# The rotation's last addition moved from VectorE to GpSimd, four per batch at fixed places of its order

## The chip, the cores and the metric

The kernel runs on one core of one Trainium2 chip. The time is that of the device in microseconds (us), the median of several executions. A core has five engines that run side by side, each its own list of instructions in order: TensorE (PE), VectorE (DVE), ScalarE (ACT), GpSimd (POOL) and SyncE (SP), which here issues the DMAs. They wait for each other by semaphores.

## What is computed

One layer of cross attention and a quantised feed-forward on x of 16 x 256 x 512, in fp32. Cut to the attention, in which the change lies:

```python
q = rope((layernorm(x) @ Wq.T + bq))     # 16 heads of 32
k = rope((ctx @ Wk.T + bk));  v = ctx @ Wv.T + bv
probs = softmax(where(causal, q @ k.T / sqrt(32), -inf))
x = x + (probs @ v) @ Wo.T + bo
x = x + ffn(layernorm(x))                # 4-bit weights, 16-bit activations
# rope: x1, x2 are the halves of a head; the result is
# [x1*c - x2*s, x1*s + x2*c]
```

## The kernel before, in words

`attend` does the attention for 16 batches of 256 tokens; `feed_forward` follows it with barriers between. In `attend` the 16 heads of a batch are four groups of four (g = 0 to 3), and s = 4 * batch + g counts the groups over all batches.

The order on every engine is written out by hand, in a string of words for each: `PE_LINE`, `ACT_LINE`, `DVE_LINE`, `POOL_LINE` (lines 81 to 87), and a `..._BEGIN` string for the opening. `whole_plan` repeats a line for i = 1 to 18. A word is a step and a group, and "+1" or "-2" shifts its batch against i: `rope1+1` in line i is the rotation of group 1 of batch i+1, `stat2-2` the second statistics of batch i-2. Words whose batch does not exist fall out. An engine works on its words strictly in that order; a word that has to wait holds up all that stand behind it.

The words of one group, in the order of the data: QK (TensorE, queries and keys of a group), raw (ScalarE, L600 and L603, adds the biases into `raw`), rope (VectorE, L504 to L512), S (TensorE, scores, L716), max (VectorE, L515 and L516), exps (ScalarE, eight exponentials, L609), recip (VectorE, L520), norm (GpSimd, L413 and L415, divides by the sums), PT (TensorE, transposes, L738 and L743), pte (ScalarE), PV (TensorE), othi and otlo (ScalarE, VectorE). There is one set of score banks: S of a group waits for the exponentials of the group before (`exped`).

A rope is four VectorE instructions on 128 x 512 fp32: `by_sin` = raw * sin, `by_cos` = raw * cos, a shuffle of `by_sin` inside each head into `sin_turned`, and the addition `qk[g]` = `by_cos` + `sin_turned`, which counts up `rotated`; S waits for `rotated`.

GpSimd's other words: stat (statistics of the layer norm of x, four small operations, L371 to L375, after VectorE's bn), stat2 (the same for the second layer norm, after x2), res (x + bias, L402) and wdeq (a unit of feed-forward weights, L407; VectorE's wqa, wqb and wqc come before it). ScalarE's xn (L583) waits for stat, xn2 (L631) for stat2. xn0 and xn1 free the tile `x_in`, into which SyncE loads the next batch (L297); bn0 (L491) waits for that load.

The order of GpSimd's steady line is, for line i:

```python
POOL_LINE = "stat2-2 stat+2 norm3-1 norm0 res-1 wdeq norm1 norm2"
```

Of the kernel before, what the change touches and what calls it, by code (L numbers as in the profile page):

```python
# [5 lines left out]
ALU = mybir.AluOpType  # L6
# [18 lines left out]
GROUPS = HEADS // HG  # L25
# [11 lines left out]
HALF_TURN = [(k + HD // 2) % HD for k in range(HD)]  # L37
# [35 lines left out]
def split_scales(dve, link, dst_inv, dst_half, peak, power):  # L73
# [10 lines left out]
            "cthi1+2 ytev1-2 exps2 pte1 xthi0+2 raw1+1 whi othi1 pte2 exps3 othi2 xthi1+2 xn1+3 raw2+1")  # L84
DVE_LINE = ("otlo2-1 max0 wqb rope2 recip0 ctlo1+1 peak-2 otlo3-1 bn0+3 max1 wqc rope3 recip1 otlo0 max2 x2_0-1 "
            "rope0+1 bn1+3 xtlo0+2 recip2 x2_1-1 wlo otlo1 max3 ctlo0+2 rope1+1 recip3 wqa+1 xtlo1+2")
POOL_LINE = "stat2-2 stat+2 norm3-1 norm0 res-1 wdeq norm1 norm2"
GATE_STEPS = ("wqa", "wqb", "wqc", "wdeq", "WT", "whi", "wlo")


# [21 lines left out]
def whole_plan(begin, line, after):  # L112

    plan = steps_of_line(begin, 0)
    for i in range(1, BATCH + 3):
        for step in steps_of_line(line, i):
            plan.append(step)
            plan += after.get((i, step[0], step[1]), [])
    return plan


def counts_of(plan):

    made, count = {}, {}
    for name, g, b in plan:
        made[name] = made.get(name, 0) + 1
        count[name, g, b] = made[name]
    return count
# [8 lines left out]
             "bn0+1 bn1+1 max0 rope1 scale1 lo4 rope2 recip0 scanc1 join2 xtlo0+1 xtlo1+1 max1 scale2 lo5 ctlo0+1 ctlo1+1 "  # L137
             "rope3 recip1 bv bn0+2 bn1+2 max2 otlo0 rope0+1 bias recip2 bn0+3 bn1+3 max3 otlo1 xtlo0+2 rope1+1 recip3 "
             "ctlo0+2 xtlo1+2")
POOL_BEGIN = "stat stat+1 norm0 stat+2 norm1 norm2"  # L140
LATE_SETS = [(2 * k - 3, k) for k in range(2, BATCH // 2)]
PE_PLAN = whole_plan(PE_BEGIN, PE_LINE, {(i, "S", 2): [("MX", j, 0)] for i, j in
                                         [(i, k + 1) for i, k in LATE_SETS] + [(DOWN_SCAN + DOWN_SCANS, 9)]})
# [10 lines left out]
DVE_PLAN = whole_plan(DVE_BEGIN, DVE_LINE, DVE_AFTER)  # L154
POOL_PLAN = whole_plan(POOL_BEGIN, POOL_LINE, {})
PE_COUNT, ACT_COUNT, DVE_COUNT, POOL_COUNT = (counts_of(p) for p in (PE_PLAN, ACT_PLAN, DVE_PLAN, POOL_PLAN))
# [16 lines left out]
def attend(nc, io, keep):  # L173

    with ExitStack() as ctx:
        def buf(name, shape, dt):
            return ctx.enter_context(nc.sbuf_tensor(name, shape, dt))

        def sem(name):
            return ctx.enter_context(nc.semaphore(name))  # L180
# [7 lines left out]
        qk = qg(76, 8, F32, "p (g a t) -> p g a t", g=GROUPS, a=2)  # L188
# [25 lines left out]
        by_sin = buf("by_sin", [P, 2, SEQ], F32)  # L214
        by_cos = buf("by_cos", [P, 2, SEQ], F32)
        sin_turned = buf("sin_turned", [P, 2, SEQ], F32)
# [49 lines left out]
        filled = [sem(f"filled{b}") for b in range(RING)]  # L266
        emptied = [sem(f"emptied{b}") for b in range(RING)]
        x_hi, c_hi, c_ready, heads_hi = sem("x_hi"), sem("c_hi"), sem("c_ready"), sem("heads_hi")
        raw_used, rotated = sem("raw_used"), sem("rotated")
        scored, max_ready, exped, sums_ready = sem("scored"), sem("max_ready"), sem("exped"), sem("sums_ready")  # L270
        normed = sem("normed")
        w_in, w_rounded, w_hi = sem("w_in"), sem("w_rounded"), sem("w_hi")
# [14 lines left out]
        def await_free(eng, name, g, b, part=0):  # L287
            bank, n = BANK[name, g, b, part]
            eng.wait_ge(emptied[bank], n + 1)
            return bank  # L290
# [71 lines left out]
        @block.gpsimd  # L362
        def _(pool):
            steps = Tally()

            def link(ins):
                ins.then_inc(pool_step, 1)
                pool.wait_ge(pool_step, steps.next())

            def statistics(mo, rs, sh):  # L370
                pool.tensor_scalar(rs[:, :], mo[:, :, 1], LN_EPS, None, ALU.add).then_inc(pool_step, 1)  # L371
                steps.next()
                link(pool.tensor_scalar(sh[:, :], mo[:, :, 0], -1.0, None, ALU.mult))
                link(pool.tensor_tensor(rs[:, :], rs[:, :], minus_half[:, :], ALU.pow))
                return pool.tensor_tensor(sh[:, :], sh[:, :], rs[:, :], ALU.mult)  # L375

            link(pool.memset(ident[:, :], 0.0))
            link(pool.memset(ident_b[:, :], 0.0))
            link(pool.memset(mask[:, :], 0.0))
            link(pool.memset(minus_half[:, :], -0.5))  # L380
            pool.memset(ones[:, :], 1.0).then_inc(ident_ready, 1)
            pool.affine_select(out=ident[:, :], in_=ident[:, :], compare_op=ALU.not_equal, fill=1.0,
                               base=0, pattern=[[-1, P]], channel_multiplier=1).then_inc(ident_ready, 1)
            for name, g, i in POOL_PLAN:
                if name == "stat":
                    pool.wait_ge(var_ready, TT * (i + 1))
                    statistics(moments, rstd, shift).then_inc(stat_ready, 1)
                    if i == 0:
                        pool.affine_select(out=ident_b[:, :], in_=ident_b[:, :], compare_op=ALU.not_equal, fill=1.0,
                                           base=0, pattern=[[-1, P]], channel_multiplier=1).then_inc(ident_ready, 1)  # L390
                        for at in (0, P):
                            diag = mask[:, at:at + P]
                            pool.affine_select(out=diag, in_=diag, compare_op=ALU.is_ge, fill=MASKED,
                                               base=0, pattern=[[-1, P]], channel_multiplier=1).then_inc(ident_ready, 1)
                if name == "stat2":
                    pool.wait_ge(x2_ready, TT * (i + 1))
                    statistics(moments2, rstd2, shift2).then_inc(stat2_ready, 1)
                if name == "res":
                    pool.wait_ge(res_loaded, 16 * (i + 1))
                    if i == 0:  # L400
                        await_free(pool, "BIAS", 0, 0)
                    pool.tensor_tensor(x_res[:, :, :], x_res[:, :, :],  # L402
                                       bias_row[:, :].unsqueeze(1).to_broadcast([P, TT, D]), ALU.add).then_inc(xb_ready, 1)
                if name == "wdeq":
                    pool.wait_ge(w_rounded, i)
                    q = w_deq[:, :].rearrange("p (k j) -> p k j", j=QBLOCK)
                    pool.tensor_tensor(q, q, step[:, :].unsqueeze(2).to_broadcast([P, D // QBLOCK, QBLOCK]),  # L407
                                       ALU.mult).then_inc(w_dequantised, 1)
                if name == "norm":
                    s = i * GROUPS + g  # L410
                    pool.wait_ge(sums_ready, s + 1)
                    pr, ps = prob[:, s % 2], per_sum[:, s % 2]
                    pool.tensor_tensor(pr[:, :, 0:P], pr[:, :, 0:P],  # L413
                                       ps[:, 0, :].unsqueeze(2).to_broadcast([P, HG, P]), ALU.mult)
                    pool.tensor_tensor(pr[:, :, P:3 * P], pr[:, :, P:3 * P],  # L415
                                       ps[:, 1, :].unsqueeze(2).to_broadcast([P, HG, 2 * P]), ALU.mult).then_inc(normed, 1)

        @block.vector
        def _(dve):
            done = Tally()  # L420

            def link(ins):
                ins.then_inc(dve_step, 1)
                dve.wait_ge(dve_step, done.next())

            for name, g, i in DVE_PLAN:
                s = i * GROUPS + g
# [76 lines left out]
                if name == "rope":  # L504
                    await_free(dve, "QK", g, i)
                    if s == 0:
                        dve.wait_ge(consts_in, 16 * 3)
                    link(dve.tensor_tensor(by_sin[:, :, :], raw[:, s % 2], sin[:, :, :], ALU.mult))
                    dve.tensor_tensor(by_cos[:, :, :], raw[:, s % 2], cos[:, :, :], ALU.mult).then_inc(raw_used, 1)
                    link(dve.stream_shuffle(sin_turned[:, :, :].rearrange("p a t -> p (a t)"),  # L510
                                            by_sin[:, :, :].rearrange("p a t -> p (a t)"), HALF_TURN))
                    dve.tensor_tensor(qk[:, g], by_cos[:, :, :], sin_turned[:, :, :], ALU.add).then_inc(rotated, 1)  # L512
                if name == "max":
                    dve.wait_ge(scored, s + 1)
                    dve.tensor_reduce(neg_max[:, s % 2, 0, :], score_banks[:, :, 0:P], AX.X, ALU.max, negate=True)  # L515
# [951 lines left out]
```

## Time and profile before

| | |
|---|---|
| median of 3 runs | 1614.03 us (1614.02 to 1615.21) |
| the profiled execution | 1613.66 us |
| its span, first to last instruction | 1611.8 us |
| mean granted clock of TensorE | 0.947 |
| TensorE busy | 1394.6 us, 87% |
| VectorE busy | 1235.3 us, 77% |
| ScalarE busy | 921.6 us, 57% |
| GpSimd busy | 321.2 us |

The profile is one execution. Busy times are sums over an engine's instructions; an engine that is idle waits for what the profile names behind "<-" in square brackets, with the idle time in front of it. In the timelines each row is one instruction or a run of equal ones: when it starts, how long it takes, the engine, the line of the code, the operation, what it writes and reads, and the shapes. The attention stage covers about the first 720 us.

### The profile page before, as it was taken

How to read it: one execution, taken by the hardware profiler on the slowest of the kernel's cores; microseconds unless marked ns; L12 is line 12 of the kernel's file. 1: busy time of each engine (PE TensorE's matmuls, PEld its weight loads, DVE VectorE, ACT ScalarE, POOL GpSimd, SP SyncE). 2: the span in 40 equal slices, each digit the busy share in tenths (PEclk: the TensorE clock that was granted, in tenths of full speed). 3: DMA queues.
4: the chain of work that ended last, by engine and by line, in shares of the span. 5: the costliest groups of instructions: out<-in, count | busy, mean ns of one | idle time of the engine just before them, and what ended most of it. 6: DMA issues, size and time to landing. Idle time of an engine off the chain costs nothing.

```text
span 1611.8 us, 24568 instructions
## 1 busy us (share of the span) xinstructions
PE 1394.6 (87%) x9268; PEld 788.2 (49%) x9268; DVE 1235.3 (77%) x2002; ACT 921.6 (57%) x1994; POOL 321.2 (20%) x326
## 2 busy tenths in 40 slices
PE   4679999999999999967999998999999103999999
PEld 3356666666666667643444444444444001444444
DVE  6657788889898988756888776788899889745641
ACT  2557777777777778755222222899844796321210
POOL 1124444444444444540111110000000000000000
PEclk9879999999999999988999999999999555999999
DMA  5101111111122121111233333577655894534532
GB/s 202 66 8 64 50 65 62 60 65 63 65 79 80 66 80 53 41 42 64 97 113 118 118 112 119 184 250 250 228 183 176 320 356 166 203 137 158 193 132 79
DMA packets 84982, 200.05 MB, mean 124 GB/s; under 512 B 8065, under 2 KB 8065, under 8 KB 84865
## 3 DMA queue, kind: packets, MB, share of 16 engines
q1 hardware_dynamic: 84864, 198.48, 35.2%
q8 instruction: 74, 1.21, 0.3%
q14 instruction: 44, 0.35, 0.1%
HBM read 128.19 MB, written 70.25 MB: 123 GB/s over the span
## 4 chain that ended last, share of the span: by engine, by line
PE 47%; issue 6%; DVE 2%; ACT 0%; POOLq 0%; POOL 0%
PE ffn_banks L1092 31%; PE ffn_banks L1110 16%; PE ffn_banks L1068 1%; DVE ffn_wide L1251 0%; DVE ffn_peaks L1258 0%; DVE ffn_rises L1256 0%; DVE ffn_wide L1250 0%; DVE qg L1351 0%; ACT ffn_rest L1150 0%; ACT ffn_ring L1141 0%; DVE ffn_wide L1385 0%; ACT qg L1150 0%; PE ffn_banks L1098 0%; DVE ffn_wide L1398 0%; DVE ffn_wide L1392 0%
## 5 line engine op out<-in xcount | busy, mean ns | idle before, releaser
L1092 PE MATMUL ffn_banks<-ffn_wide,ffn_rest 128*128 128x512 f16 x2304 | 506.2, 381 | 10.4 <-DVE ffn_wide L1251 6.1
L1092 PEld LDWEIGHTS ffn_banks<-ffn_wide,ffn_rest 128*128 128x128 f16 x2304 | 226.2, 98 | 280.9 <-issue 17.1
L1110 PE MATMUL ffn_banks<-ffn_rest,ffn_wide 128*128 128x512 f16 x1152 | 251.4, 382 | 103.3 <-DVE ffn_wide L1392 103.3
L609 ACT ACTIVATE qg<-score_banks,neg_max 128x128 f32<-128x128 f32 (+1 forms) x512 | 208.0, 446 | 52.8 <-DVE neg_max L516 52.8
L1110 PEld LDWEIGHTS ffn_banks<-ffn_rest,ffn_wide 128*128 128x128 f16 x1152 | 113.3, 98 | 241.4 <-issue 107.2
L1150 ACT ACTIVATE ffn_rest<-ffn_banks,ffn_row_back 128x1024 f32<-128x1024 f32 x72 | 79.7, 1107 | 155.6 <-PE ffn_banks L1092 145.9
L1222 ACT ACTIVATE ffn_u_steps<-ffn_ring,ffn_scales 128x1024 int16<-128x1024 f32 x48 | 55.1, 1149 | 154.2 <-DMA ffn_ring<-ups_dram 135.4
L413 POOL TENSOR_TENSOR qg<-qg,per_sum 128x512 f32<-128x512 f32 x64 | 70.1, 1095 | 306.5 <-DVE per_sum L520 306.5
L415 POOL TENSOR_TENSOR qg<-qg,per_sum 128x1024 f32<-128x1024 f32 x64 | 121.1, 1892 | 0.0
L609 ACT ACTIVATION_READ_ACCUMULATOR qg<-score_banks,neg_max 128x1 f32 x512 | 119.1, 233 | 0.0
L657 PE MATMUL ring_banks<-xt,attn_hi 128*128 128x256 f16 x512 | 89.8, 277 | 10.2 <-DVE ct L501 6.2
L616 ACT ACTIVATE pt<-ring_banks 128x512 f32<-128x512 f32 x128 | 71.0, 609 | 42.0 <-PE ring_banks L738 41.4
L738 PE MATMUL ring_banks<-ident,qg 128*128 128x128 f32 x512 | 70.8, 280 | 27.9 <-POOL qg L415 14.0
L1258 DVE TENSOR_REDUCE ffn_peaks<-ffn_rest 128x1 f32<-128x1024 f32 x72 | 87.3, 1213 | 8.2 <-ACT ffn_rest L1150 8.1
L657 PE MATMUL ring_banks<-ct,attn_hi 128*128 128x256 f16 x512 | 89.2, 276 | 0.0
L657 PE MATMUL ring_banks<-attn_hi,ot 128*128 128x512 f16 x256 | 81.8, 382 | 0.5
L657 PE MATMUL ring_banks<-attn_hi,ct 128*128 128x512 f16 x256 | 82.1, 383 | 0.0
L1150 ACT ACTIVATE qg<-ffn_banks,ffn_row_back 128x1024 f32<-128x1024 f32 x24 | 26.7, 1114 | 94.3 <-PE ffn_banks L1092 94.3
L516 DVE TENSOR_REDUCE neg_max<-score_banks 128x4 f32<-128x1024 f32 x64 | 77.7, 1215 | 0.0
L1391 DVE CAST ffn_wide<-ffn_wide 128x1024 f16<-128x1024 int16 x48 | 20.5, 427 | 74.2 <-PE ffn_banks L1110 72.7
L738 PEld LDWEIGHTS ring_banks<-ident,qg 128*128 128x128 f32 x512 | 58.4, 143 | 37.6 <-POOL qg L415 20.4
L1233 POOL TENSOR_TENSOR ffn_ring<-ffn_ring,ffn_step 128x512 f32<-128x512 f32 x24 | 25.1, 1048 | 239.9 <-DVE ffn_ring L1285 239.9
(178 smaller groups left out, 2718.9 us busy)
## 6 DMA issues: line engine op xcount, KB each, us to landing
ffn_ring<-ups_dram SPq DMA_DIRECT2D x60, 512.0 KB, 4.1
ups_dram<-ffn_rest SPq DMA_DIRECT2D x48, 512.0 KB, 3.0
ffn_wide<-ups_dram SPq DMA_DIRECT2D x33, 512.0 KB, 9.4
gates_dram<-ffn_rest SPq DMA_DIRECT2D x24, 512.0 KB, 2.7
ffn_ring<-gates_dram SPq DMA_DIRECT2D x24, 512.0 KB, 4.6
ffn_rest<-w_parts_dram SPq DMA_DIRECT2D x36, 256.0 KB, 4.0
x_in<-in_x SPq DMA_DIRECT2D x16, 512.0 KB, 3.7
qg<-in_ctxt SPq DMA_DIRECT2D x16, 512.0 KB, 4.3
```

Of the source, the lines that this page charges most:

```text
L413: pool.tensor_tensor(pr[:, :, 0:P], pr[:, :, 0:P], ps[:, 0, :].unsqueeze(2).to_broadcast([P, HG, P]), ALU.mult)
L415: pool.tensor_tensor(pr[:, :, P:3 * P], pr[:, :, P:3 * P], ps[:, 1, :].unsqueeze(2).to_broadcast([P, HG, 2 * P]), ALU.mult).then_inc(norme ...
L516: dve.tensor_reduce(neg_max[:, s % 2, 1, :], score_banks[:, :, P:3 * P], AX.X, ALU.max, negate=True).then_inc(max_ready, 1)
L609: last = act.activation(prob[:, s % 2, h, lo:hi], score_banks[:, h, lo:hi], ACT.Exp, bias=neg_max[:, s % 2, part, h:h + 1], accum_out=row_ ...
L616: act.activation(pt0[:, 2 * part:2 * part + 2, :], banks[:, b, :].rearrange("p (h q) -> p h q", h=2), ACT.Copy).then_inc(emptied[b], 1)
L657: last = pe.matmul(out, a, m, start=(k == 0), stop=(k == count - 1))
L738: last = pe.transpose(banks[:, b, h * SEQ + q * P:h * SEQ + (q + 1) * P], prob[:, s % 2, 2 * part + h, q * P:(q + 1) * P], ident[:, :])
L1092: last = pe.matmul(banks[:, pair_of(s), half, :], w[:, m % 2, wp, c, :], xq[:, xp, n, c, :], start=(k == 0), stop=(k == 3 * DC - 1))
L1110: last = pe.matmul(down_banks[:, g % 2, t, :], oq[:, g % 2, op, m, t * P:(t + 1) * P], w_down[:, wp, wk, c], start=(start and k == 0), sto ...
L1150: act.activation(stage_of(s), banks[:, pair_of(s)].rearrange("p h n -> p (h n)"), ACT.Copy, scale=row_back[:, s // PIECES:s // PIECES + 1] ...
L1222: act.activation(du_steps[:, r % 2], du[:, r % 4], ACT.Copy, scale=sc["u_per"]).then_inc(du_rounded, 1)
L1258: dve.tensor_reduce(peaks[:, s:s + 1], stage_of(s), AX.X, ALU.max, apply_absolute_value=True).then_inc(peaked, 1)
```

## The change

GpSimd gets four words per batch, add0 to add3, each the addition of one group. VectorE's rope ends with the shuffle, which counts up a new semaphore `turned`; `raw_used` still counts the cosine product. GpSimd's add waits for both and counts up `rotated`. Because the next rope writes `by_sin`, `by_cos` and `sin_turned` again, it first waits until the add before it is done (`rotated` at s).

```diff
-POOL_LINE = "stat2-2 stat+2 norm3-1 norm0 res-1 wdeq norm1 norm2"
+POOL_LINE = "stat2-2 stat+2 norm3-1 add2 norm0 res-1 wdeq add3 norm1 add0+1 norm2 add1+1"
-POOL_BEGIN = "stat stat+1 norm0 stat+2 norm1 norm2"
+POOL_BEGIN = "stat add0 stat+1 add1 add2 norm0 stat+2 add3 norm1 add0+1 norm2 add1+1"
...
+                if name == "add":
+                    s = i * GROUPS + g
+                    pool.wait_ge(turned, s + 1)
+                    pool.wait_ge(raw_used, s + 1)
+                    pool.tensor_tensor(qk[:, g], by_cos[:, :, :], sin_turned[:, :, :], ALU.add).then_inc(rotated, 1)
...
                     if s == 0:
                         dve.wait_ge(consts_in, 16 * 3)
+                    else:
+                        dve.wait_ge(rotated, s)
                     link(dve.tensor_tensor(by_sin[:, :, :], raw[:, s % 2], sin[:, :, :], ALU.mult))
                     dve.tensor_tensor(by_cos[:, :, :], raw[:, s % 2], cos[:, :, :], ALU.mult).then_inc(raw_used, 1)
-                    link(dve.stream_shuffle(sin_turned[:, :, :].rearrange("p a t -> p (a t)"),
-                                            by_sin[:, :, :].rearrange("p a t -> p (a t)"), HALF_TURN))
-                    dve.tensor_tensor(qk[:, g], by_cos[:, :, :], sin_turned[:, :, :], ALU.add).then_inc(rotated, 1)
+                    dve.stream_shuffle(sin_turned[:, :, :].rearrange("p a t -> p (a t)"),
+                                       by_sin[:, :, :].rearrange("p a t -> p (a t)"), HALF_TURN).then_inc(turned, 1)
```

## Rows read from the trace of the kernel before

**Rows 1.** The page, busy time by engine.

```profile
PE 1394.6 (87%) x9268; PEld 788.2 (49%) x9268; DVE 1235.3 (77%) x2002; ACT 921.6 (57%) x1994; POOL 321.2 (20%) x326
```

**Rows 2.** Busy time by stretch: stretch, length, engines, granted clock, DMA share, GB/s.

```profile
400.00:560.00 160.00, 147.78 (x1395) 104.12 (x1394) 142.08 (x260) 124.47 (x387) 75.36 (x72) 1.00 0.22 74
```

**Rows 3.** Waits of 80 to 720: us in total, times, longest.

```profile
PE score_banks L724 <- ACT qg L609: 22.9, 15, 2.8
...
PE ring_banks L738 <- POOL qg L415: 14.0, 10, 5.5
```

**Rows 4.** Timeline of GpSimd, between norm2 and the end of norm3.

```profile
425.12 0.22 POOL L371 TENSOR_SCALAR rstd<-moments 128x2 f32<-128x2 f32 x1
...
428.17 0.22 POOL L375 TENSOR_TENSOR shift<-shift,rstd 128x2 f32<-128x2 f32 x1
431.41 1.04 POOL L413 TENSOR_TENSOR qg<-qg,per_sum 128x512 f32<-128x512 f32 x1 [3.02 <-DVE per_sum L520]
432.40 1.89 POOL L415 TENSOR_TENSOR qg<-qg,per_sum 128x1024 f32<-128x1024 f32 x1
```

**Rows 5.** Timeline of VectorE, the end of rope1+1.

```profile
429.59 0.74 DVE L510 STREAM_SHUFFLE sin_turned<-by_sin 128x512 f32<-128x512 f32 x1
430.36 0.69 DVE L512 TENSOR_TENSOR qg<-by_cos,sin_turned 128x512 f32<-128x512 f32 x1
```

**Rows 6.** Timeline of ScalarE, xn1+3 and the start of pte3.

```profile
431.80 0.81 ACT L583 ACTIVATE xn<-x_in,shift,rstd 128x512 f32<-128x512 f32 x1
...
435.55 0.60 ACT L616 ACTIVATE pt<-ring_banks 128x512 f32<-128x512 f32 x1
```

**Rows 7.** Timeline of TensorE: S2, PT1 and PT3.

```profile
410.85 0.50 PE L724 MATMUL score_banks<-qg 32*128 32x128 f32 x8 [1.91 <-ACT qg L609]
...
416.01 1.09 PE L738 MATMUL ring_banks<-ident,qg 128*128 128x128 f32 x8 [1.09 <-POOL qg L415]
...
434.92 1.04 PE L738 MATMUL ring_banks<-ident,qg 128*128 128x128 f32 x8
```

**Rows 8.** Groups of GpSimd's instructions, 80 to 720: count, busy, mean ns, idle.

```profile
L402 POOL TENSOR_TENSOR x_res<-x_res,bias_row 128x1024 f32<-128x1024 f32 x16 | 37.8, 2365 | 38.4 <-DMA x_res<-in_x 38.4
...
L407 POOL TENSOR_TENSOR w_deq<-w_deq,step 128x512 f32<-128x512 f32 x12 | 17.1, 1426 | 14.5 <-DVE w_deq L562 14.5
```

**Rows 9.** Timelines of VectorE and GpSimd around rope3, norm1 and norm2.

```profile
410.08 1.42 DVE L509 TENSOR_TENSOR by_cos<-qg,cos 128x512 f32<-128x512 f32 x1
...
411.43 0.72 DVE L510 STREAM_SHUFFLE sin_turned<-by_sin 128x512 f32<-128x512 f32 x1
...
413.06 1.04 POOL L413 TENSOR_TENSOR qg<-qg,per_sum 128x512 f32<-128x512 f32 x1 [2.11 <-DVE per_sum L520]
...
422.14 1.04 POOL L413 TENSOR_TENSOR qg<-qg,per_sum 128x512 f32<-128x512 f32 x1 [6.19 <-DVE per_sum L520]
```

**Rows 10.** Timelines of ScalarE and VectorE: xn0+2 and bn0+3.

```profile
400.15 0.89 ACT L583 ACTIVATE xn<-x_in,shift,rstd 128x512 f32<-128x512 f32 x1
...
404.72 0.69 DVE L491 BATCH_NORM_STATS2 stats<-x_in 128x6 f32<-128x512 f32 x1 [2.65 <-DMA x_in<-in_x]
```

**Rows 11.** Stretches as in rows 2, and transposes at the lower clock.

```profile
167.60:171.40 3.80, 3.78 (x24) 2.00 (x25) 1.89 (x5) 2.77 (x6) 2.89 (x2) 0.55 0.02 4
...
690.00:700.00 10.00, 9.77 (x61) 6.01 (x62) 6.66 (x20) 5.64 (x22) 4.49 (x4) 0.83 0.01 2
...
95.68 1.76 PE L738 MATMUL ring_banks<-ident,qg 128*128 128x128 f32 x8 [1.85 <-ACT qg L603]
```

**Rows 12.** Timelines: rope1+1's shuffle and norm3, in lines 2 and 14.

```profile
145.52 0.75 DVE L510 STREAM_SHUFFLE sin_turned<-by_sin 128x512 f32<-128x512 f32 x1
...
147.41 1.04 POOL L413 TENSOR_TENSOR qg<-qg,per_sum 128x512 f32<-128x512 f32 x1 [1.70 <-DVE per_sum L520]
...
632.98 0.74 DVE L510 STREAM_SHUFFLE sin_turned<-by_sin 128x512 f32<-128x512 f32 x1
...
634.79 1.04 POOL L413 TENSOR_TENSOR qg<-qg,per_sum 128x512 f32<-128x512 f32 x1 [4.59 <-DVE per_sum L520]
```

More of the change, by code:

```diff
@@ L268, in attend @@
         x_hi, c_hi, c_ready, heads_hi = sem("x_hi"), sem("c_hi"), sem("c_ready"), sem("heads_hi")
-        raw_used, rotated = sem("raw_used"), sem("rotated")
+        raw_used, turned, rotated = sem("raw_used"), sem("turned"), sem("rotated")
         scored, max_ready, exped, sums_ready = sem("scored"), sem("max_ready"), sem("exped"), sem("sums_ready")
```

## The prediction

> **What bounds the kernel now.** I read the page first, then the busy time by stretches, then the waits of the attention stage, then the timelines of one batch, engine by engine. The page says that TensorE is busy for 87% of the 1611.8 us [rows 1]. The change touches only the attention stage, roughly 80 to 720 us, where one batch takes about 40.7 us in the steady part. There TensorE is busy for 147.8 of 160 us and VectorE for 142.1 [rows 2], so neither average decides; the order does. TensorE's longest waits with a named cause are scores waiting for the exponentials of the group before (15 times, 22.9 us) and the probability transposes waiting for GpSimd's normalisation (10 times, 14.0 us) [rows 3]. What a moved addition costs is therefore read from what stands behind it in the queues.
>
> I follow line i = 9, the batch around 400 to 440 us. Names are those of the plans: rope, norm, stat, PT and so on, with "+1" for the next batch.
>
> **VectorE's side: what is removed.** Each rope loses its addition, 0.69 us [rows 5], and the wait on the shuffle in front of it, some 0.04 us: 64 x 0.73 = 47 us less on VectorE. On the path almost nothing of it counts. rope1+1, the last of the line, follows max3, which waits for the scores S3; TensorE reaches S3 through a full queue. The other three are followed by work that waits for something else: in the line's first part VectorE stands at bn0+3 until x_in has landed (xn0+2 at 400.15, batch statistics at 404.72 after 2.65 us idle) [rows 10]. So VectorE gains time mostly in front of waits.
>
> **GpSimd's side: the price of one addition.** The trace has no 128x512 addition of two full fp32 operands on GpSimd. Nearest is x_res + bias, two full operands of 1024: 2.365 us on average [rows 8]. The two halves of norm, 1.04 us for 512 and 1.89 for 1024 [rows 4], put the fixed part at 0.19 us, which gives (2.36 - 0.19) / 2 + 0.19 = 1.27 us. The bounds are 1.04 us, norm's first half, and 1.43 us, the de-quantising product of the same size [rows 8]. I take 1.27, as its row reads two full operands. (The Trainium skill, GPSIMD Engine Reference, section 3.1, gives about 2.6 cycles per element for a two-input operation at 1.2 GHz, an estimate of 1.11 us. With it the sum below would be some 4 us lower.)
>
> **Three additions fit, nearly.** add2 stands between norm3-1 and norm0; rope2's shuffle ends well before the exponentials that norm0 needs. add0+1 stands in the 6.19 us for which GpSimd is idle between norm1's end, at 415.95, and norm2's start, at 422.14 [rows 9]: hidden. If that cover went, each would cost at most its 1.27 us. add3 is different: norm1 follows it, and PT1 starts at 416.01, 0.06 us after norm1's end [rows 7]. Now the shuffle of rope3 ends at 412.15 and norm1 starts at 413.06 [rows 9]. Afterwards the addition starts at 412.23, ends at 413.50, and norm1 starts then: 0.4 us later. TensorE waited for norm1 here in ten to eleven lines: 11 x 0.4 = 4.4 us.
>
> **add1+1 does not fit.** It is the last word of GpSimd's line, and GpSimd works in order. Behind it stand the next line's stat2-2 and stat+2 and then norm3-1. Today the statistics run in the gap after norm2: first operation at 425.12, the last ends at 428.39, 3.27 us for the two sets. GpSimd is then idle for 3.02 us and starts norm3 at 431.41 [rows 4]. The shuffle of rope1+1 ends only at 430.33 [rows 5]. So afterwards:
> - add1+1 runs 430.41 to 431.68;
> - the two sets of statistics run 431.77 to 435.04;
> - norm3 runs 435.1 to 438.0 (2.88 us, as now), where it now ends at 434.29.
>
> Two engines wait for that. ScalarE has xn1+3 next at 431.80 [rows 6], which needs stat+2: it stands until 435.1, +3.3 us, and behind it in its queue are raw2+1, xn2_0, xn2_1, Vev0, pte3 and then exps0, all of which follow without a gap now (pte3 at 435.55 [rows 6]). TensorE has PT3 at 434.92 [rows 7], which needs norm3: it starts at 438.05, +3.1 us, with 3 us of idle that does not exist today. pte3 needs both: ScalarE is ready at 435.55 + 3.3 = 438.85 and the first bank is full by then, so exps0 comes 3.3 us late.
>
> **Is it made good later in the line?** S1 waits for exps0. xn0+2 follows exps0 on ScalarE, and the load of x_in follows xn0+2; bn0+3 waits for that load and max1 stands behind bn0+3 [rows 10]; exps1 follows max1, and S2 waits for exps1 (1.91 us of idle in this line) [rows 7]. Each link is tight today, so the 3.3 us arrive whole at S2, and from there TensorE's full queue carries them to S3, max3 and rope1+1, which closes the loop. The line becomes 3.3 + 0.4 us longer.
>
> **How many lines.** Both statistics are in lines 2 to 13, twelve of them, each with the same picture: from the shuffle's start to norm3's is 1.9 us in line 2 (145.52 and 147.41) and 1.8 us in line 14 (632.98 and 634.79) [rows 12]. 12 x 3.3 = 39.6 us. Lines 14 and 15 have only stat2: the addition ends at 635.05, the statistics take 1.6 us, norm3 runs 636.8 to 639.7, and PT3 comes 1.4 us late: 2.7 us for the two. Line 1 and the opening have longer waits on TensorE around them; I put them at nothing (at most 2 us). The feed-forward is untouched.
>
> **The clock.** TensorE's new idle time stands between the short scores and the transposes. Of seven waits of 2.0 to 2.2 us before S2, two were followed by a fall from 2.4 to 1.2 GHz: granted clock 0.55 over the 3.8 us from 167.6, and 0.83 over the ten from 690; the other five kept the full clock [rows 11]. A wait of 3 us comes before PT3 now; I let the clock fall in half of the twelve lines. Eight transposes took 1.76 us at the lower level (at 95.68) [rows 11] and 1.04 at the upper [rows 7]; for the twelve of PT3 that is 1.08 us more, some 1.0 of it on the path: 6 x 1.0 = 6 us. (The Trainium skill, TensorE: Matmul & The Clock Gate, "Why this matters for your kernels", warns of idle gaps of about this length between bursts. That rule speaks against the change; the trace agrees so far as the two falls show it.)
>
> **The sum.** 39.6 + 4.4 + 2.7 + 6 = 52.7 us on the profiled execution's 1613.66 us (span 1611.8 and 1.9 around it), so 1666.4. The median of the runs is 0.4 us above the profiled one. I predict 1666 us, 3.2% slower.
>
> **Rivals.**
> - *The waits of today take up part of it.* TensorE idles 1.0 to 2.1 us in front of S2 in most lines. If exps1 did not move with the stall, that idle would shrink first and a line would grow by about 1.6 us: 12 x 1.6 + 7 = 26 us, 1640. Against it: the load of x_in starts from xn0+2, which is itself late [rows 10]. Chance 0.12.
> - *The clock falls in every line* and TensorE loses about 1.7 us each time: 46.7 + 12 x 1.7 = 67 us, 1681. For it: the idle stretch is longer than any of the seven. Chance 0.14.
> - *The shared port.* by_cos took 1.42 us where it started beside a GpSimd product, against 0.69 for an instruction of the same form with GpSimd idle [rows 5, 9], so an addition on GpSimd can hold up VectorE's instructions with two operands, ctlo1+1 behind rope2 above all. Price: the rest of the addition, up to 0.5 us, or of a norm right behind it, 2.9 us, in each of 14 lines; at the 0.5 end the total is 1673, at the other it is beyond 1685. (The Trainium skill, SBUF — State Buffer, "Who interferes with whom", calls this an exclusive lock held for the whole instruction; the 1.42 agrees.) Against it: after the stall add2 is over 2 us before recip0 and ctlo1+1 come. Chance of a cost that shows: 0.05.
> - *Faster, because VectorE decides after all.* If the 0.73 us saved per rope, 2.9 us a line, carried rope1+1 forward, the addition and the statistics would be back in the gap, and recip1, released 0.7 us earlier in 11 lines, would bring up to 8 us: 1606. It decides when the shuffle of rope1+1 ends over 3.1 us earlier against S3. Against it: rope1+1 stands behind max3, and max3 behind TensorE. Chance 0.04.
> - *No effect that can be told:* the queued statistics turn out to be covered. 1614, chance 0.03.
>
> **Chances and range.** Forecast 0.62, with its own range 1652 to 1678 (the addition at 1.04 or 1.43 us moves the sum by -6 or +4, no clock fall takes off 6). About 0.2% is what a measurement of this kernel can tell from no change. Faster 0.04, within 0.2% 0.03, slower 0.93. The 8-in-10 range leaves out the faster and unchanged cases (0.07), the lower half of the partly absorbed one and the top of the clock and port cases: 1645 to 1685.
>
> **What would show each step.** In the profile after: GpSimd's addition near 1.27 us; the statistics behind add1+1 and not behind norm2; ScalarE idle about 3.3 us before xn1+3 with GpSimd as the cause; TensorE idle about 3 us before PT3, released by norm; a batch of 44 to 45 us instead of 40.7; the granted clock below 1.0 in some of those places; VectorE's busy time down by some 44 us and its idle up by more. The prediction is wrong if rope1+1 ends much earlier in its line, if the wait at S2 has vanished, or if the batch has kept its length.

## The result

The changed kernel takes 1664.99 us in the median (1661.15 to 1666.06), against 1614.03 before: a ratio of 1.031, 95% interval 1.0293 to 1.0327. It is 51 us slower. The profiled execution took 1661.15 us, with a span of 1659.4; it is the quickest of the four, and 47.5 us above the profiled execution of before.

Busy time by engine, from the page of the changed kernel:

```profile
PE 1410.6 (85%) x9268; PEld 796.2 (48%) x9268; DVE 1201.9 (72%) x1938; ACT 924.1 (56%) x1994; POOL 396.1 (24%) x390
```

Beside [rows 1], VectorE has lost 33 us of work and GpSimd has gained 75. The additions, in the groups of the same page (count, busy, mean ns, idle before):

```profile
L413 POOL TENSOR_TENSOR qg<-by_cos,sin_turned 128x512 f32<-128x512 f32 x64 | 81.8, 1278 | 239.0 <-DVE sin_turned L517 239.0
```

Their median is 1.272 us; the forecast took 1.27. One batch boundary of the changed kernel follows, the counterpart of the one in [rows 4 to 7]. First GpSimd's timeline:

```profile
410.27 1.27 POOL L413 TENSOR_TENSOR qg<-by_cos,sin_turned 128x512 f32<-128x512 f32 x1 [5.37 <-DVE sin_turned L517]
411.62 0.22 POOL L371 TENSOR_SCALAR rstd<-moments 128x2 f32<-128x2 f32 x1
...
414.69 0.19 POOL L375 TENSOR_TENSOR shift<-shift,rstd 128x2 f32<-128x2 f32 x1
414.83 1.04 POOL L418 TENSOR_TENSOR qg<-qg,per_sum 128x512 f32<-128x512 f32 x1
415.83 1.89 POOL L420 TENSOR_TENSOR qg<-qg,per_sum 128x1024 f32<-128x1024 f32 x1
```

GpSimd is now idle for 5.4 us in front of add1+1, where it did the statistics before. Behind the addition come the statistics and norm3 without a gap: the work has not grown much, it has been queued. ScalarE and TensorE, in their timelines of the same place, show who waits for it:

```profile
414.91 0.81 ACT L589 ACTIVATE xn<-x_in,shift,rstd 128x512 f32<-128x512 f32 x1 [3.14 <-POOL shift L375]
...
413.46 0.50 PE L730 MATMUL score_banks<-qg 32*128 32x128 f32 x8
...
417.78 1.09 PE L744 MATMUL ring_banks<-ident,qg 128*128 128x128 f32 x8 [2.83 <-POOL qg L420]
```

From the first score of the batch (413.46) PT3 starts 4.3 us later; before, 434.92 - 433.60 = 1.3. The wait of 2.81 to 2.83 us before PT3 stands in all twelve lines, 2 to 13. In lines 14 and 15 it is 1.16 and 0.94.

Where the 47.5 us of the profiled execution lie, by the start of each batch's first scores:

| | before | changed |
|---|---|---|
| first scores of batch 1 | 110.47 | 109.01 |
| from batch 1 to batch 15 | 563.56 | 610.10 |
| from batch 15 to the end of the span | 937.8 | 940.3 |
| a batch, mean of batches 4 to 8 | 40.71 | 44.18 |

So 46.5 us are in the fourteen batches, the opening is 1.5 us shorter, and the tail is 2.5 us longer. The 1.5 us say nothing about the change: in four profiles of kernels with this same opening, batch 1 started between 107.1 and 109.4. The tail can be taken apart. The last PT3 comes 1.35 us later behind batch 15's first scores (38.39 us, before 37.04). From it to VectorE's last addition of x it takes 12.4 us in place of 10.8, although the work is the same. The rest of the span, the feed-forward, is 0.5 us shorter. In front of the last PT3 both kernels wait for 5.48 us, and behind it the clock is low in both, but not for equally long (columns as in [rows 2], from the start of that PT3 to the end of the last output matmuls, before and then changed):

```profile
711.00:721.90 10.90, 9.98 (x60) 6.04 (x60) 2.08 (x5) 3.26 (x6) 2.33 (x2) 0.87 0.00 0
757.50:769.90 12.40, 11.58 (x60) 7.11 (x60) 2.05 (x5) 3.37 (x6) 2.25 (x1) 0.71 0.00 0
```

### The profile page after: what moved, and what is told of

Read it like the earlier page. It is cut to its first block, busy times and chain, and to the rows that moved or that the text cites. A ratio compares the mean times of both kernels' runs of the same rounds, so it can differ in the third digit from the quotient of the medians.

```text
span 1659.4 us, 24683 instructions
## 1 busy us (share of the span) xinstructions
PE 1410.6 (85%) x9268; PEld 796.2 (48%) x9268; DVE 1201.9 (72%) x1938; ACT 924.1 (56%) x1994; POOL 396.1 (24%) x390
## 4 chain that ended last, share of the span: by engine, by line
PE 45%; issue 6%; DVE 2%; ACT 0%; POOLq 0%; POOL 0%
PE ffn_banks L1098 30%; PE ffn_banks L1116 15%; PE ffn_banks L1074 1%; DVE ffn_wide L1257 0%; DVE ffn_peaks L1264 0%; DVE ffn_rises L1262 0%; DVE ffn_wide L1256 0%; DVE qg L1357 0%; ACT ffn_rest L1156 0%; ACT ffn_ring L1147 0%; DVE ffn_wide L1391 0%; ACT qg L1156 0%; PE ffn_banks L1104 0%; DVE ffn_wide L1404 0%; DVE ffn_wide L1398 0%
## 5 line engine op out<-in xcount | busy, mean ns | idle before, releaser
L1116 PEld LDWEIGHTS ffn_banks<-ffn_rest,ffn_wide 128*128 128x128 f16 x1152 | 113.3, 98 | 241.3 <-issue 107.1
L413 POOL TENSOR_TENSOR qg<-by_cos,sin_turned 128x512 f32<-128x512 f32 x64 | 81.8, 1278 | 239.0 <-DVE sin_turned L517 239.0
L663 PE MATMUL ring_banks<-attn_hi,ct 128*128 128x512 f16 x256 | 87.2, 404 | 0.0
```

What stands on the lines that cost most here:

```text
L413: pool.tensor_tensor(qk[:, g], by_cos[:, :, :], sin_turned[:, :, :], ALU.add).then_inc(rotated, 1)
L663: last = pe.matmul(out, a, m, start=(k == 0), stop=(k == count - 1))
L1116: last = pe.matmul(down_banks[:, g % 2, t, :], oq[:, g % 2, op, m, t * P:(t + 1) * P], w_down[:, wp, wk, c], start=(start and k == 0), sto ...
```

## The experiments

Each kernel is the changed one with the edit shown. Medians; the ratio is to the kernel before on the same chip. Its median was 1613.16 us beside the first four (up to the wait without an addition), 1614.5 beside norm3 first, half of the queue and add3 behind norm1, 1613.26 beside the additions done twice, the changed kernel once more and the filled wait, and 1614.97 beside the last two. The text in front of each result is what was expected before it ran.

**The order, with all additions on GpSimd.** The statistics go back in front of add1+1.

```diff
-POOL_LINE = "stat2-2 stat+2 norm3-1 add2 norm0 res-1 wdeq add3 norm1 add0+1 norm2 add1+1"
+POOL_LINE = "norm3-1 add2 norm0 res-1 wdeq add3 norm1 add0+1 norm2 stat2-1 stat+3 add1+1"
-POOL_BEGIN = "stat add0 stat+1 add1 add2 norm0 stat+2 add3 norm1 add0+1 norm2 add1+1"
+POOL_BEGIN = "stat add0 stat+1 add1 add2 norm0 stat+2 add3 norm1 add0+1 norm2 stat+3 add1+1"
```

> All four additions stay on GpSimd; only the two sets of statistics are moved in front of add1+1, back into the gap behind norm2. Theory (the loss is the order: statistics and norm3 queued behind add1+1): the wait of 2.8 us before PT3 and ScalarE's wait before xn1+3 vanish, norm3 starts some 0.3 us later than in the kernel before, which its 0.6 us of slack covers; what is left is add3 in front of norm1, 11 x 0.4 = 4 us: 1616 to 1621 us. Rival (GpSimd's additions cost by themselves, by the shared port or by S waiting for the slower addition): most of the 51 us stays, above 1645. Rival (VectorE's 2.9 us a batch now pay): below 1611.

Measured: 1618.67 us, ratio 1.0032 (1.002 to 1.0045). Nine tenths of the loss are gone though every addition is still on GpSimd. GpSimd's and then TensorE's timeline at the boundary:

```profile
430.65 0.21 POOL L375 TENSOR_TENSOR shift<-shift,rstd 128x2 f32<-128x2 f32 x1
432.88 1.27 POOL L413 TENSOR_TENSOR qg<-by_cos,sin_turned 128x512 f32<-128x512 f32 x1 [2.02 <-DVE sin_turned L517]
434.10 1.05 POOL L418 TENSOR_TENSOR qg<-qg,per_sum 128x512 f32<-128x512 f32 x1
...
436.07 0.50 PE L730 MATMUL score_banks<-qg 32*128 32x128 f32 x8
...
437.38 1.04 PE L744 MATMUL ring_banks<-ident,qg 128*128 128x128 f32 x8
```

PT3 has no wait and is 1.3 us behind the first score, as in [rows 7]. The rival by which GpSimd's additions cost by themselves falls.

**One addition, and the other three.** Group 1 alone on GpSimd, and then all but group 1; the rest is added by VectorE. For the first:

```diff
-POOL_LINE = "stat2-2 stat+2 norm3-1 add2 norm0 res-1 wdeq add3 norm1 add0+1 norm2 add1+1"
+POOL_LINE = "stat2-2 stat+2 norm3-1 norm0 res-1 wdeq norm1 norm2 add1+1"
-POOL_BEGIN = "stat add0 stat+1 add1 add2 norm0 stat+2 add3 norm1 add0+1 norm2 add1+1"
+POOL_BEGIN = "stat stat+1 add1 norm0 stat+2 norm1 norm2 add1+1"
...
+                    if g != 1:
+                        dve.wait_ge(turned, s + 1)
+                        dve.tensor_tensor(qk[:, g], by_cos[:, :, :], sin_turned[:, :, :], ALU.add).then_inc(rotated, 1)
```

> Only group 1's addition is on GpSimd, at its place at the line's end; groups 0, 2 and 3 are added by VectorE as before. Theory: 12 lines x 3.0 us and 2.6 us for lines 14 and 15, without add3's 4 us and with fewer clock falls than twelve: 1652 to 1658 us. Rival (every addition on GpSimd bears a part): a quarter of the 51 us, 1627.

Measured: 1660.0 us, ratio 1.0286 (1.0258 to 1.0314), 2 us above the range expected; the clock fell in ten of its twelve lines (below). The second has the words add1 taken out and the condition `g == 1`.

> Groups 0, 2 and 3 on GpSimd, group 1 added by VectorE, so nothing stands in front of the statistics. Theory: add0 and add2 hidden, add3 costs 0.4 us in 11 lines: 1616 to 1620 us. Rival (every addition bears a part): 1652. The sum of the differences of this and of the one with group 1 alone should be near 51 us.

Measured: 1619.66 us, ratio 1.0031 (1.0017 to 1.0044). The differences are 46.8 and 6.5 us, together 53, near the 51 of the whole. Group 1's addition carries the loss, and the three others together cost about 6 us. That it is the place and not the addition is for the next experiment.

**The wait without an addition.** All additions on VectorE; GpSimd only waits at add1+1's place.

```diff
                 if name == "add":
                     s = i * GROUPS + g
-                    pool.wait_ge(turned, s + 1)
-                    pool.wait_ge(raw_used, s + 1)
-                    pool.tensor_tensor(qk[:, g], by_cos[:, :, :], sin_turned[:, :, :], ALU.add).then_inc(rotated, 1)
+                    pool.wait_ge(rotated, s + 1)
```

with the orders of group 1 alone, and VectorE adding every group.

> All additions are VectorE's, GpSimd adds nothing; it only waits, at add1+1's place, until VectorE's rotation of that group is done. Theory (order): GpSimd goes on at the end of VectorE's addition, 0.7 us behind the shuffle in place of 1.3, so statistics and norm3 come some 2.5 us late in 12 lines and 0.8 us in two: 1614 + 30 + 2 = 1646 us, PT3 idle about 2.3 us. Rival (GpSimd's time or the port): no addition, no loss, 1614.

Measured: 1651.13 us, ratio 1.0228 (1.0201 to 1.0255). GpSimd has no addition at all and 38 of the 51 us are there. Its timeline, and TensorE's:

```profile
451.90 0.22 POOL L371 TENSOR_SCALAR rstd<-moments 128x2 f32<-128x2 f32 x1 [6.10 <-DVE qg L519]
...
455.12 1.04 POOL L416 TENSOR_TENSOR qg<-qg,per_sum 128x512 f32<-128x512 f32 x1
...
458.07 1.97 PE L745 MATMUL ring_banks<-ident,qg 128*128 128x128 f32 x8 [2.22 <-POOL qg L418]
459.83 1.06 PE L750 MATMUL ring_banks<-ident,qg 128*128 128x128 f32 x4
```

The wait before PT3 is 2.22 us where 2.3 was expected. The time is 5 us above the expected one; the same rows show a cause: the eight transposes take 1.97 us here and 1.09 in the changed kernel at 417.78. The section on the clock returns to this.

**ScalarE or TensorE.** norm3 in front of the statistics, both behind add1+1.

```diff
-POOL_LINE = "stat2-2 stat+2 norm3-1 add2 norm0 res-1 wdeq add3 norm1 add0+1 norm2 add1+1"
+POOL_LINE = "norm3-1 stat2-2 stat+2 add2 norm0 res-1 wdeq add3 norm1 add0+1 norm2 add1+1"
```

> The changed kernel with norm3-1 in front of the two sets of statistics, behind add1+1. It tells TensorE's wait for norm3 from ScalarE's wait for the statistics. Theory (ScalarE's xn1+3 and the words behind it carry the delay too): norm3 comes 0.3 us late only, but the statistics end near 437.9 in place of 435.0, so xn1+3 is 6.1 us late, raw2+1 behind it holds the bank that PT3 needs, and the line grows by 6 us and more: 1685 to 1705 us. Rival (only norm3 before PT3 matters): as with the statistics first, 1617 to 1621.

Measured: 1704.12 us, ratio 1.055 (1.0524 to 1.0577). norm3 is on time and the kernel is slower still. GpSimd's, ScalarE's and TensorE's timelines:

```profile
477.57 1.04 POOL L418 TENSOR_TENSOR qg<-qg,per_sum 128x512 f32<-128x512 f32 x1
...
484.36 0.81 ACT L589 ACTIVATE xn<-x_in,shift,rstd 128x512 f32<-128x512 f32 x1 [6.50 <-POOL shift L375]
...
486.23 1.09 PE L744 MATMUL ring_banks<-ident,qg 128*128 128x128 f32 x4 [5.20 <-ACT qg L609]
```

PT3's data are there at 480.5. It waits until 486.2 for a free bank, which raw2+1 (L609) empties, and raw2+1 stands behind xn1+3, which waits for the statistics. norm3 is not what TensorE waits for here; the delay of the statistics reaches it through ScalarE's queue.

**Half of the queue.** One set of statistics back in front of add1+1, stat2 left behind it.

```diff
-POOL_LINE = "stat2-2 stat+2 norm3-1 add2 norm0 res-1 wdeq add3 norm1 add0+1 norm2 add1+1"
+POOL_LINE = "stat2-2 norm3-1 add2 norm0 res-1 wdeq add3 norm1 add0+1 norm2 stat+3 add1+1"
```

> The changed kernel with one of the two sets, that of x for xn, moved in front of add1+1, and stat2 left behind it. Theory: the delay is proportional to what stands between add1+1 and norm3: norm3 ends near 436.3, PT3 is 1.4 us late in 14 lines, xn1+3 is on time: 1614 + 20 + 4 = 1638 us. Rival (only ScalarE's xn1+3 matters): 1618.

Measured: 1636.44 us, ratio 1.0131 (1.0113 to 1.0149). PT3 waits 1.16 to 1.18 us in the twelve lines and starts 1.3 us later against S0 than before (2.65 us behind it, before 1.32), where 1.4 was expected; the stretch from 300 to 600 us has the full clock. ScalarE does xn1+3, raw2+1 and both xn2 without a wait and stands for 1.43 us only at pte3, which needs PT3: this is the other branch, norm3 alone.

**The two hidden additions.** add0 and add2 are done twice.

```diff
+                    if g in (0, 2):
+                        link(pool.tensor_tensor(qk[:, g], by_cos[:, :, :], sin_turned[:, :, :], ALU.add))
                     pool.tensor_tensor(qk[:, g], by_cos[:, :, :], sin_turned[:, :, :], ALU.add).then_inc(rotated, 1)
```

> The changed kernel with the additions of groups 0 and 2 done twice on GpSimd (the same result), 2 x 1.3 us more per batch at the two places said to be hidden. Theory: they lie beside waits, the time stays within 2 us of the changed kernel beside it. Rival (every addition on GpSimd costs its time): 14 x 2.7 = 38 us more. If one of the two places is tight, 14 x 1.3 = 18 us more.

Measured: 1664.7 us, beside 1665.35 for the changed kernel: 2 x 1.3 us of GpSimd's time per batch cost nothing there.

**The clock.** First the changed kernel once more:

> The changed kernel itself once more, beside the two below on the same chip: 1661 to 1667 us.

Measured: 1665.35 us (1663.4 to 1666.38), ratio 1.0317 (1.0302 to 1.0333). Then with matmuls in the wait:

```diff
                 if name == "PT":
+                    if g == 3 and 1 <= i <= 12:
+                        b = open_bank("PT", g, i, 1)
+                        for _ in range(40):
+                            pe.matmul(banks[:, b, 0:P], ident_b[:, :], mask[:, 0:P], start=True, stop=True)
                     pe.wait_ge(normed, s + 1)
```

> The changed kernel with 40 additional small matmuls (128 columns, bf16) per line in TensorE's wait before PT3 in the twelve lines, into a ring bank that PT3 overwrites; the output is unchanged. Theory (a part of the loss is the clock that falls around this wait): the granted clock stays at 1.0 there, the longer batches (45.2 to 46.0 us) shrink towards 44.2, and the time drops by 2 to 6 us below the changed kernel beside it. Rival (the falls cost nothing on the path): within 1 us of it. If the matmuls overrun the wait, PT3 starts behind norm3's end and the time rises; the profile shows it.

Measured: 1656.64 us, five runs from 1656.40 to 1656.77; ratio to before 1.0265 (1.025 to 1.028). TensorE does 480 matmuls more and the kernel is 8.7 us quicker, more than the 2 to 6 us expected. TensorE's timeline:

```profile
501.66 2.40 PE L742 MATMUL ring_banks<-mask,ident_b 128*128 128x128 bf16 x40
504.65 1.09 PE L748 MATMUL ring_banks<-ident,qg 128*128 128x128 f32 x8 [0.60 <-POOL qg L420]
505.58 0.60 PE L753 MATMUL ring_banks<-ident,qg 128*128 128x128 f32 x4
```

For comparison, the changed kernel where the clock fell. Two stretches, one up to and one behind the start of PT3 (columns as in [rows 2]):

```profile
504.60:508.00 3.40, 0.57 (x6) 0.42 (x5) 3.21 (x3) 3.28 (x6) 2.93 (x3) 1.00 0.00 0
508.00:512.00 4.00, 4.00 (x18) 2.15 (x16) 2.12 (x5) 4.00 (x15) 1.26 (x1) 0.59 0.00 0
```

and the second half of PT3 in its timeline:

```profile
508.51 0.84 PE L749 MATMUL ring_banks<-ident,qg 128*128 128x128 f32 x4
```

In the stretch of the wait TensorE was busy for 0.57 us at the full clock; in the next the granted clock is 0.59 on average, so most of it is at 1.2 GHz, and PT3's last four transposes take 0.84 us in place of 0.60. Such lines can be told by the distance from the first scores S0 to S1: 12.3 to 12.4 us with the full clock, 13.8 to 15.2 with a fall (9.3 before the change). By this count the clock fell in 6 of 12 lines in the first profile of the changed kernel, in 9 of 12 in the second, and in none of the 12 with the matmuls in the wait. With the additions done twice it fell in 9, with group 1 alone in 10 (12.2 to 12.4 us without a fall), and with the wait alone in 10 (11.7 us without, 13.2 to 13.4 with). With norm3 first, where the wait is 4.7 to 5.2 us, it fell in all twelve; with one set of statistics ahead, where it is 1.2 us, in none. In the filled kernel PT3 starts 4.3 us behind the first score, as in the changed one, so the falls come from TensorE's idling and not from the later start.

What a fall costs comes out between 0.7 and 0.9 us. The profiled executions of the pair are 8.6 us apart (1664.99 and 1656.40), but only 6.0 of that lie between the first scores of batch 1 and of batch 15, where the twelve lines are: 0.7 us for each of 9 falls. The rest, 1.5 us in the opening and 1.1 in the tail, is not the filled waits' doing. And in the second profile of the changed kernel batches 6 to 10, each with a fall, last 45.1 us on average, and batches 4, 5 and 11, without one, 44.2. (The Trainium skill, TensorE: Matmul & The Clock Gate, "Why this matters for your kernels", advises against idle gaps of over about 3 us between bursts. Here waits of 2.2 and 2.8 us with short scores in front and transposes behind were enough in many lines, and one of 1.2 us in none.)

**A version that beats both.** The statistics first, and add3 behind norm1.

```diff
-POOL_LINE = "stat2-2 stat+2 norm3-1 add2 norm0 res-1 wdeq add3 norm1 add0+1 norm2 add1+1"
+POOL_LINE = "norm3-1 add2 norm0 res-1 wdeq norm1 add3 add0+1 norm2 stat2-1 stat+3 add1+1"
-POOL_BEGIN = "stat add0 stat+1 add1 add2 norm0 stat+2 add3 norm1 add0+1 norm2 add1+1"
+POOL_BEGIN = "stat add0 stat+1 add1 add2 norm0 stat+2 norm1 add3 add0+1 norm2 stat+3 add1+1"
```

> All four additions on GpSimd, the statistics in front of add1+1, and add3 behind norm1 in place of in front of it. Theory: nothing is queued in front of work that TensorE waits for; recip1 comes some 0.7 us earlier than in the kernel before, norm1 and PT1 with it, for 10 to 11 lines: 1604 to 1610 us, faster than before. What could take it back: rope0+1 waits for add3, which now ends some 1.2 us behind norm1, 0.3 us later than rope0+1 starts today; that is hidden if rope0+1 has slack. Rival (VectorE's saved time has no use anywhere): 1613 to 1616.

Measured: 1608.51 us, ratio 0.9965 (0.9952 to 0.9977). Once more beside the last experiment:

> The kernel with the statistics first and add3 behind norm1 once more, beside the one above on the same chip: 1606 to 1611 us, 4 to 8 us below the kernel before.

Measured: 1607.75 us, ratio 0.9959 (0.9944 to 0.9974). That is 6 to 7 us below the kernel before, from the same four additions on GpSimd. In front of PT1 the waits of 0.5 to 1.1 us are nearly all gone. It is less than the 0.7 us times 11 of VectorE's side; in the first profile batches 4 to 12 take 365.7 us together and in the second 365.5, before 369.0, so 0.4 us each. Another 2.5 us lie in the opening (first scores of batch 1 at 108.0 and 108.2 in place of 110.5). As equal openings differ by up to 2.3 us, and the kernel before has one profile, that part isn't shown to be the change's. Part of what is missing can be seen on ctlo1+1, VectorE's instruction behind rope2 and recip0. Its group before, and in this kernel (mean ns behind the busy time):

```profile
L501 DVE SCALAR_TENSOR_TENSOR ct<-qg,inv,ct 128x512 f16<-128x512 f32 x28 | 23.8, 851 | 0.2
```

```profile
L506 DVE SCALAR_TENSOR_TENSOR ct<-qg,inv,ct 128x512 f16<-128x512 f32 x28 | 27.4, 980 | 0.2
```

add2 pushes norm0 back by 0.3 us, and ctlo1+1, with two operands from SBUF, stands until norm0's half is done: 3.6 us over 28 instructions. One of the long ones in the timelines of GpSimd and VectorE, 1.61 us, which ends 0.54 us behind norm0:

```profile
438.87 1.90 POOL L420 TENSOR_TENSOR qg<-qg,per_sum 128x1024 f32<-128x1024 f32 x1
439.70 1.61 DVE L506 SCALAR_TENSOR_TENSOR ct<-qg,inv,ct 128x512 f16<-128x512 f32 x1
```

(The Trainium skill, SBUF — State Buffer, "Who interferes with whom": such an instruction and a GpSimd instruction that reads exclude each other for the whole instruction. The rows agree.) In every other line bn0+3 and max1 stand close behind it, and exps1 starts 14.8 us after S0 in place of 14.5.

**Every addition behind a norm.** The last experiment tried to take that back.

```diff
-POOL_LINE = "norm3-1 add2 norm0 res-1 wdeq norm1 add3 add0+1 norm2 stat2-1 stat+3 add1+1"
+POOL_LINE = "norm3-1 add1 norm0 add2 res-1 wdeq norm1 add3 add0+1 norm2 stat2-1 stat+3"
-POOL_BEGIN = "stat add0 stat+1 add1 add2 norm0 stat+2 norm1 add3 add0+1 norm2 stat+3 add1+1"
+POOL_BEGIN = "stat add0 stat+1 add1 add2 norm0 stat+2 norm1 add3 add0+1 norm2 stat+3"
```

> All four additions on GpSimd, the statistics right behind norm2, and the additions of groups 1, 2 and 3 each behind the norm that follows in time (norm3, norm0, norm1) instead of in front of it. Against the kernel with the statistics first and add3 late (1608.5 us): norm0 starts 0.3 us earlier in the lines where add2 pushed it, so ctlo1+1 is held up less (its mean back from 0.98 to 0.85 us) and exps1 comes 0.3 us earlier in six lines: 2 us less, 1605 to 1609 us. Rival (the additions now come too late for the next rope or the next scores): 1612 and more, with VectorE waiting before rope2 or rope3.

Measured: 1611.17 us, ratio 0.998 (0.9971 to 0.9989). ctlo1+1 is back at 0.851 us and exps1 at 14.5 in those lines, both as expected, and yet the time is outside the 1605 to 1609 us expected and 3.4 us above the kernel beside it (their intervals overlap slightly). In its profile w_deq's rounding (L566) takes 1.086 us on average, in the other 0.968, and lines 13 and 14 are 0.6 us longer with 0.47 us of wait before PT1. No experiment ties these together; where the 3.4 us come from is open.

## Why the prediction was right, step by step

- **The price of one addition**: 1.27 taken from x_res + bias and the fixed part of norm, 1.272 measured.
- **add1+1 does not fit**: right in place, cause and size. norm3's end was forecast 3.7 us later in its line and is 3.6 us later (417.72 - 413.46, before 434.29 - 433.60); PT3's wait was forecast at 3 us and is 2.81 to 2.83 in exactly the twelve lines named. The experiments separate the order from the addition: statistics first, 5.5 us left; wait alone, 38 us.
- **Two engines wait**: shown. xn1+3 starts 3.2 us later against S0 (414.91 - 413.46, before 431.80 - 433.60), with 3.14 us of idle. The 3.3 us became 3.1 at exps0 (6.48 us after S0, before 3.40), since pte3 had a little slack. The order with norm3 first shows that ScalarE's branch alone holds TensorE up, and the one with half of the queue shows it for norm3's.
- **Nothing is made good later**: S2 comes 3.1 us late against S0 (21.1, before 18.0) and still waits 1.0 to 2.1 us for exps1 in lines without a fall. The rival by which that wait is used up first falls.
- **add3 in front of norm1**: PT1 waits 1.47 us at 439.97, before 1.09 at 416.01 [rows 7], and 0.98 where it was 0.5: the 0.4 us forecast. The number of lines was read a little wrong: PT1 waits for norm1 in nine lines of the trace before (batches 4 to 12), not in ten to eleven, and in twelve of the changed kernel (3 to 14). A line without a fall is 3.47 us longer, where 3.7 was forecast.
- **The two hidden additions**: shown by doing them twice.
- **The clock**: that the wait before PT3 makes the clock fall in a part of the lines was right, and half of the lines was right for the profiled execution; the second profile had nine falls. The price was forecast at 1.0 us and is 0.7 to 0.9. That half of the lines would fall had little to rest on: of the seven waits counted two fell, and a wait of 2.80 us before S2 at 128.30 in the same trace, as long as the one forecast, kept the full clock and was not counted. Without falls the changed kernel is 43.4 us slower (1656.64 against 1613.26), where the sum without its clock term said 46.7.
- **Lines 14 and 15**: forecast at 2.7 us. Line 14 is 1.7 us longer (38.76, before 37.04), and line 15 is late by 1.35 at its end.
- **The opening and the tail**: put at nothing. The opening's 1.5 us are within what equal openings differ by. Of the tail's 2.5 us, 1.35 belong to line 15. Another 1.6 are the longer time at the low clock behind the last PT3, whose wait of 5.48 us the kernel before has too; the same stretch takes 10.8 us in some profiles and 12.4 or more in others, 12.7 in one of the quick kernel with add3 behind norm1, which has no wait before the other PT3. So it isn't shown to be the change's. The feed-forward itself is 0.5 us shorter.

The sum of 52.7 us was made of one term too large by 0.2 us a line and a clock term that happened to be near. The sum and the median agree to within 2 us, the profiled execution and the sum to 5; that the median is so close is in part luck, as these errors cancel.

The rival of the shared port costs nothing that can be seen in the changed kernel's time, and for ctlo1+1 it is for the reason given: after the stall add2 is over before ctlo1+1 comes (mean 0.852 us, before 0.851). But the prediction missed another instruction that is held up, wqb, in front of rope2. Its group before, and in the changed kernel, and then VectorE's next wait behind one of them (which starts at 416.72 and takes 1.55 us, beside norm3 until 417.72):

```profile
L556 DVE TENSOR_TENSOR w_deq<-w_raw,per_step 128x512 f32<-128x512 f32 x12 | 8.2, 682 | 0.0
```

```profile
L562 DVE TENSOR_TENSOR w_deq<-w_raw,per_step 128x512 f32<-128x512 f32 x12 | 16.8, 1403 | 0.0
```

```profile
423.33 0.20 DVE L526 RECIPROCAL per_sum<-row_sum 128x8 f32<-128x8 f32 x1 [2.96 <-ACT qg L615]
```

It is the late norm3 that does it, in ten of twelve, and the 0.9 us vanish in the 2.96 us for which VectorE waits for exps0. It is also the main reason why VectorE's busy time fell by 33 us, where the prediction said some 44: the additions took 44.3 us with them, and wqb alone gave 8.7 back. Once the stall is taken away, the rival's cost on ctlo1+1 does show, at 3.6 us of VectorE's time in all. The rival by which VectorE's saved time decides is true only of a kernel with another order: 6 to 7 us, against the 8 at most that were forecast.

## What to carry to other kernels

When a step moves to another engine, its place in that engine's queue matters more than its duration: look at what is queued behind it, when its input arrives, and who waits for what stands behind. Here the engine was 80% idle and the moved step cost 51 us behind the wrong neighbours and gained 6 in a better order. Put the moved step behind work whose input is earlier, and count a wait on TensorE twice: for itself and for the clock that may fall after it (here 3.1 us and, in half of the lines or more, another 0.7 to 0.9).

## What was not expected

- Filling a wait with useless matmuls pays: 40 of them, 2.40 us, in a wait of 2.8 us removed every fall in the twelve lines and took 6.0 us off the fourteen batches. The five runs of that kernel lie within 0.4 us, the four of the changed one beside it within 3. The falls before PT3 alone don't explain that: the kernel before, without them, spread over 6.4 us in 19 runs (1610.86 to 1617.23). Its trace has falls behind other waits, of 2.1 us before S2 at 167.6 and 690.2, and of 5.5 us before the last PT3, and the filled kernel keeps such waits too. Why its runs lie so close is open.
- The length of the wait alone does not say whether the clock falls. With waits of 2.8 us (in three lines of one profile 2.4) the falls were 6, 9, 9 and 10 of 12 in four profiles, with 2.1 to 2.2 us 10 of 12 in one; 4.7 to 5.2 us gave twelve and 1.2 us none.
- A GpSimd instruction that runs beside no VectorE instruction of two operands can still hold VectorE up, by moving the next GpSimd instruction by 0.3 us onto one that has them.
